# A gated cross-attention megakernel: the ternary layer written into the attention heads' plan, weights loaded first

## The chip, the cores and the metric

The kernel runs on one core of one Trainium2 chip, as one launch. The metric is the time of that launch on the device, in microseconds (us): 1436.66 us, the median of three runs (1432.61 to 1437.38). PE is TensorE, DVE is VectorE, ACT is ScalarE, POOL is GpSimd and SP is SyncE, whose queue issues most DMAs.

## What is computed

Two transformer-like layers on x of 16 tiles with 128 rows of 512 numbers, in float32. The change touches only the first layer, that is the first two lines of four:

```
x = x + tanh(g_xattn[0]) * heads(layernorm(x), ctx, mask)        # 16 heads of 32, 128 keys a tile
x = x + tanh(g_ffn[0])   * ternary(layernorm(x), weight, bias)   # one 512x512 layer
x = x + tanh(g_xattn[1]) * features(layernorm(x), ctx)           # sigmoid attention over features
x = x + tanh(g_ffn[1])   * experts(layernorm(x))                 # routing, 16 experts, shared expert

heads:   x = rmsnorm(h) * norm_w ; q = x wq', k = ctx wk', v = ctx wv'
         softmax(q k' / sqrt(32), masked) v ; then out wo' * sigmoid(x wg')
ternary: xn = x / rms(x); gamma = mean|weight| per output row
         w3 = clip(round(weight / (gamma + eps)), -1, 1)
         s  = max|xn| / 127 per row of x;  xq = clip(round(xn / (s + eps)), -127, 127)
         out = (xq w3') * gamma * s + bias
```

## The kernel before

The tensor x lies in SBUF as X, 16 tiles of 128x512. The stages run one after another, each as a block of the five engines' programs, and a block ends for all engines together.

**Start of the heads (lines 300 to 383, 449 to 470).** SP loads the five weights into two raw buffers in turn (qT and kT, not yet in use), so the third load waits until the first weight has been transposed; between them stand the loads of X (four of 1 MB), of two context tiles and of the masks. PE transposes each weight by 16 transposes into four PSUM banks (L351), ACT writes the high half of each quarter (L367) and DVE the low half (L211): a float32 number is used as a sum of two float32r halves, and `mm3` (lines 60 to 64) makes one product of three matmuls. After that a prologue does the first pair's transposes and the projections k and q.

**The heads' loop.** Tiles go in groups of four (GB = 4, NG = 4). One string, `plan` (lines 231 to 238), sets the order of a group, the same for all engines. A word is a step: `Sa`, `Sb` the scores of half a tile (four heads in each of two banks), `sm` the softmax of a quarter (DVE maximum L694, subtraction L699, ACT exponential L602, DVE row sums L707, one sum pass for two quarters), `pT` the transposes of the probabilities (PE L427, ACT L557), `pv` their product with v, `rc` and `bc` the reciprocals of the sums and their broadcast by PE, `on` and `oT` the normalised output and its halves, `v`, `g`, `oP`, `q`, `k` the projections, `xT`, `cT` the transposes of a tile of normalised x and of context (PE L427, ACT L555, DVE L627). PE writes transposes to two banks T in turn and projections to two banks M in turn; whoever is two steps later in the same bank waits until it has been read. Each engine executes in order. PE's program is written out for four groups (`for g in range(NG)`, L472); ACT, DVE, POOL and SP run a hardware loop of four turns (`Fori`), with register arithmetic ahead of each wait. As a loop's turn is the same for every g, the last turn also transposes and projects tiles of a next group, which wraps round to the first tiles and is never used.

**The ternary stage (`ternary_ffn`, lines 738 to 944).** A block of its own. DVE makes the means and scales of all 16 tiles (`row_scale`, lines 113 to 131, with two powers on POOL, L139 and L142), and the ternary weights (L809 to L822). Then it goes in pairs of tiles: normalise (L829), maximum (L832), three small steps (L836 to L838), round (L843), PE transposes (L917), ACT to bf16 (L893), PE four matmuls a tile (L941), DVE the product with the scales (L854), POOL two additions to X (L876 the bias, L881 the product), DVE the statistics for the next normalisation (L859).

Of the kernel before, what the change touches and what calls it, by code (L numbers as in the profile page):

```python
# [66 lines left out]
def program(nc, x, ctx_in, mask, g_x, g_f, norm_w, wq, wk, wv, wo, wg, fw, fb,  # L67
            gate_w, ebias, w1, w2, w3, sw1, sw2, sw3, out):
    with ExitStack() as top:
        def sb(name, shape, dt=F32):  # L70
# [74 lines left out]
def attention_heads(nc, c, x, g_x, g_f, fw, ctx_in, mask, norm_w, wq, wk, wv, wo, wg):  # L145

    X, identF = c["X"], c["identF"]
    with ExitStack() as st:
# [9 lines left out]
        W = [sb(f"W{n}", [P, 2, KC, D], F32R) for n in "qkvgo"]  # L158
        WQ, WK, WV, WG, WO = W
# [15 lines left out]
        rs = sb("rs", [P, D])  # L175
# [3 lines left out]
        upd = sb("upd", [P, 2, D])  # L179
        mask_u8 = sb("mask_u8", [NB, S], U8)  # L180
        mask_f = sb("mask_f", [NB, S])
        mask_all = sb("mask_all", [P, NB, S], U8)
        T, M, SC = bank("T", 2), bank("M", 2), bank("SC", 2)
        O, REC = bank("O", 1)[0], bank("REC", 1)[0]


        raw = [t_[:, :, :, :].rearrange("p a k t -> p (a k t)").rearrange("p (o k) -> p o k", o=KC) for t_ in (qT, kT)]
        names = [(WQ, wq, "norm"), (WK, wk, None), (WV, wv, None), (WG, wg, "norm"), (WO, wo, "gate")]

        def scale_of(how, kc):  # L190

            return nw[:, kc:kc + 1] if how == "norm" else hg[:, 0:1] if how == "gate" else 1.0
        w_in = [sem(f"w_in{i}") for i in range(2)]
        nw_in, mask_in, w_tr, w_hi, w_lo = sem("nw_in"), sem("mask_in"), sem("w_tr"), sem("w_hi"), sem("w_lo")
        powered, m_ready, m_tr, m_col, scales = sem("powered"), sem("m_ready"), sem("m_tr"), sem("m_col"), sem("scales")
        hg_ready, tg_ready, gates_bc = sem("hg_ready"), sem("tg_ready"), sem("gates_bc")
        x_in, g_in = [sem(f"x_in{q}") for q in range(NG)], sem("g_in")
        zeroed, consts, seen = sem("zeroed"), sem("consts"), sem("seen")

        def rows_stats(dve, q):  # L200
            dve.wait_ge(x_in[q], 16)
            for t in range(q * GB, (q + 1) * GB):
# [24 lines left out]
        plan = steps("Sa.0 xT.1.0 Sb.0 sm.0 sm.1 v.0 cT.1.0 xT.1.1 g.0 pT.0 cT.1.1 q.1.0 Sa.1 pT.1 Sb.1 sm.2 sm.3 "
# [7 lines left out]

        prologue = [(n, 2, i) for n, count in (("cT", GB // 2), ("k", KC), ("xT", GB // 2), ("q", KC)) for i in range(count)]  # L240

        T_KINDS, M_KINDS = ("xT", "cT", "pT"), ("q", "k", "v", "g", "oP")
        SPLIT, BY_ACT, BY_DVE = ("xT", "cT"), ("q", "k", "g"), ("v", "oP")

        def of(kinds, steps=None):
            return [s for s in (plan if steps is None else steps) if s[0] in kinds]

        def at(kinds, s):


            back = 0
            if s[0] in ("xT", "cT", "q", "k") and s[1] == 0:
                s, back = (s[0], 2, s[2]), 1
            elif s[0] in ("oP", "v", "g") and s[1] < 0:
                s, back = (s[0], s[1] + GB), 1
            elif s[0] == "pT" and s[1] < 0:
                s, back = (s[0], s[1] + NQ), 1
            some = of(kinds)
            return some.index(s) + 1 - back * len(some)

        def upto(kinds, sub, n):

            some = of(kinds)
            if n >= 0:
                return len([s for s in some[:n] if s[0] in sub])
            return len([s for s in some[:n] if s[0] in sub]) - len(of(sub))

        assert len(of(T_KINDS)) % 2 == 0 and len(of(M_KINDS)) % 2 == 0
        c_in = [sem(f"c_in{q}") for q in range(2)]
        mask_all_in = sem("mask_all_in")  # L270
        mrow_ready = Count(sem("mrow_ready"), GB, before=GB)
        x_norm = Count(sem("x_norm"), GB, before=2)
        t_fill = Count(sem("t_fill"), len(of(T_KINDS)), True, 4)
        t_hi = Count(sem("t_hi"), len(of(T_KINDS)), True, 4)
        t_lo = Count(sem("t_lo"), len(of(SPLIT)), True, 4)
        m_fill = Count(sem("m_fill"), len(of(M_KINDS)), True, 2 * KC)
        m_act = Count(sem("m_act"), len(of(BY_ACT)), True, 2 * KC)
        m_dve = Count(sem("m_dve"), len(of(BY_DVE)), True)
        s_fill = Count(sem("s_fill"), NQ)
        s_half = Count(sem("s_half"), NQ)  # L280
        s_out = Count(sem("s_out"), 3 * NQ, True)
        r_out = Count(sem("r_out"), GB, True)
        p_exp = Count(sem("p_exp"), NQ)
        pv = Count(sem("pv"), 3 * GB, True)
        o_norm = Count(sem("o_norm"), 2 * GB, True)
        o_hi = Count(sem("o_hi"), GB)
        o_lo = Count(sem("o_lo"), GB, True)
        added = Count(sem("added"), GB, True)
        HG = GB // 2
        GC = HG * S  # L290

# [4 lines left out]
        def tile_of(g, grp, j):  # L296

            return ((g + 1) * GB) % NB + j if grp == 2 else g * GB + grp * HG + j

        with nc.Block() as block:  # L300
            @block.sync
            def _(sp):
                sp.dma_start(gates[:, 0:2], g_x.rearrange("(a n) -> a n", a=1)).then_inc(g_in, 16)
                sp.dma_start(gates[:, 2:4], g_f.rearrange("(a n) -> a n", a=1)).then_inc(g_in, 16)
                with nc.allow_non_contiguous_dma(reason="512 scales once"):
                    sp.dma_start(nw[:, :], norm_w.rearrange("(k p) -> p k", p=P)).then_inc(nw_in, 16)
                for n, (_, w, _) in enumerate(names):
                    if n >= 2:
                        sp.wait_ge(w_tr, KC * (n - 1))
                    sp.dma_start(raw[n % 2][:, :, :], w.rearrange("(o p) k -> p o k", p=P)).then_inc(w_in[n % 2], 16)  # L310
# [1715 lines left out]
```

## Time and profile before

| what | us |
|---|---|
| median of three runs | 1436.66 |
| the profiled execution | 1438.92 |
| its span, first to last instruction | 1437.2 |
| start, to the first scores of the heads | 57.6 |
| heads' loop, four groups | 365.7 |
| from the heads' last matmul to the next stage's first transposes | 87.0 |
| all later stages | 926.9 |

In the first slice of 36 us the DMAs move 299 GB/s.

The page of the profile has a line for each engine's busy time in 40 equal slices of about 36 us: PE is at nine tenths or more in slices 3 to 11 and at four and five tenths in slices 13 and 14, where DVE is at nine. The mean granted clock of TensorE over the span is 0.94. Times in the rows are us from the span's start.

### The profile page before, as it was taken

Reading aid. Unit: us, or ns where it says so; the run is one execution under the profiler, and the core shown is the slowest. Engines: PE = TensorE matmul, PEld = TensorE weight load, DVE = VectorE, ACT = ScalarE, POOL = GpSimd, SP = SyncE. Lnnn points to the kernel's source line nnn. Section 1 sums busy time; section 2 is a strip of 40 time slices with the busy share of each in tenths; the row PEclk is TensorE's granted clock in tenths of the full one; section 3 lists DMA queues with packets and bytes.
Section 4 is the critical chain, followed back from the end, with each engine's and each line's share of the span. In section 5 each row is a group of like instructions: output and inputs, shape, how many; then the busy total and the mean of one; then the engine's idle time right before and its main releaser. Section 6 shows DMA issues by size and latency. Waiting matters only on the chain. (4 is left out here: it accounts for less than half of the span.)

```text
span 1437.2 us, 26164 instructions
## 1 busy us (share of the span) xinstructions
PE 1261.7 (88%) x7939; PEld 1058.4 (74%) x7944; DVE 761.4 (53%) x1393; ACT 521.0 (36%) x994; POOL 421.7 (29%) x487
## 2 busy tenths in 40 slices
PE   4899999999974579968997889679999989999992
PEld 3788888888863257745775677569999978998992
DVE  5555565565559979963666543334324543424340
ACT  3334333343322168843111112234334543434340
POOL 0100000000015665550003740124444434443442
PEclk8899999999997779979998999889999999999996
DMA  8000000000000011133000200356435665545456
GB/s 299 24 8 16 16 16 1 16 16 16 10 7 1 0 59 44 37 135 119 0 1 0 90 30 30 129 162 135 85 73 133 146 161 145 128 86 133 81 140 161
DMA packets 53297, 103.81 MB, mean 72 GB/s; under 512 B 4807, under 2 KB 20167, under 8 KB 53176
## 3 DMA queue, kind: packets, MB, share of 16 engines
q1 hardware_dynamic: 37608, 66.04, 14.0%
q0 software_dynamic: 15632, 36.97, 13.3%
q8 instruction: 40, 0.66, 0.2%
q14 instruction: 17, 0.14, 0.0%
HBM read 76.26 MB, written 30.93 MB: 75 GB/s over the span
## 5 line engine op out<-in xcount | busy, mean ns | idle before, releaser
L1876 PE MATMUL t_H<-m_W,t_xT 128*128 128x352 f32 x1632 | 285.7, 331 | 15.8 <-DVE m_W L1954 13.9
L1876 PEld LDWEIGHTS t_H<-m_W,t_xT 128*128 128x128 f32 x1632 | 267.2, 192 | 18.0 <-DVE m_W L1954 14.4
L1843 POOL DMA_INDIRECT acc_d<-t_ys,t_sid x68 | 109.4, 1609 | 281.7 <-ACT t_ys L1905 199.7
L408 POOL TENSOR_TENSOR X<-X,upd 128x512 f32 x16 | 20.5, 1281 | 352.1 <-DVE upd L685 352.1
L62 PE MATMUL t_Y<-m_W,t_hT 128*128 128x512 f32 (+1 forms) x207 | 88.5, 427 | 9.1 <-DVE t_hT L1999 6.1
L1921 ACT ACTIVATE t_sl<-t_H 128x352 f32<-128x352 f32 x68 | 31.5, 464 | 173.7 <-PE t_H L1876 173.7
L1975 DVE TENSOR_TENSOR t_h<-t_H,t_sl 128x352 f32<-128x352 f32 x68 | 35.6, 523 | 104.4 <-ACT t_sl L1921 98.6
L1997 DVE TENSOR_TENSOR t_hT<-t_TH,t_hT 128x256 fp32r<-128x256 f32 x68 | 28.8, 423 | 106.8 <-ACT t_hT L1942 105.7
L64 PE MATMUL t_Y<-m_W,t_hT 128*128 128x512 f32 (+1 forms) x207 | 82.8, 400 | 0.0
L63 PE MATMUL t_Y<-m_W,t_hT 128*128 128x512 f32 (+1 forms) x207 | 82.5, 398 | 0.0
L1905 ACT ACTIVATE t_ys<-t_Y,t_wcol 128x512 f32<-128x512 f32 x69 | 47.4, 686 | 95.7 <-PE t_Y L64 88.2
L1817 POOL DMA_INDIRECT t_xg<-rows_d,t_gid x72 | 71.2, 989 | 22.0 <-issue 21.8
L602 ACT ACTIVATE pr<-pr 128x512 f32<-128x512 f32 x64 | 40.4, 631 | 83.3 <-DVE pr L699 83.3
L694 DVE TENSOR_REDUCE mx<-SC 128x4 f32<-128x512 f32 x64 | 43.9, 686 | 46.8 <-PE SC L517 46.8
L1334 POOL TENSOR_SCALAR m_W<-m_W,bst 128x128 fp32r<-128x128 f32 x64 | 55.3, 883 | 27.9 <-PE eL L1398 27.8
L1729 DVE SCALAR_TENSOR_TENSOR X<-eY,tg,X 128x512 f32<-128x512 f32 x32 | 23.9, 751 | 63.3 <-PE eY L64 63.3
L557 ACT ACTIVATE pT<-T 128x512 f32<-128x512 f32 x64 | 38.1, 595 | 47.2 <-PE T L427 46.6
L1950 DVE TENSOR_TENSOR t_xT<-t_TX,t_xT 128x512 fp32r<-128x512 f32 x69 | 47.6, 690 | 12.0 <-issue 7.4
L62 PEld LDWEIGHTS t_Y<-m_W,t_hT 128*128 128x128 f32 (+1 forms) x207 | 39.5, 191 | 16.1 <-DVE m_W L1991 6.8
L699 DVE TENSOR_TENSOR pr<-SC,mx 128x512 f32<-128x512 f32 x64 | 44.3, 692 | 13.2 <-DVE mx L694 13.2
L1855 PE MATMUL t_TX<-identF,t_xg 128*128 128x128 f32 x276 | 42.3, 276 | 9.9 <-DMA t_xg<-rows_d,t_gid 9.6
L1453 ACT ACTIVATE ehT<-eh 128x512 fp32r<-128x512 f32 (+1 forms) x24 | 15.2, 632 | 97.6 <-DVE eh L1671 97.6
(379 smaller groups left out, 3263.0 us busy)
## 6 DMA issues: line engine op xcount, KB each, us to landing
m_r<-in_L_ffn_w_dram SPq DMA_DIRECT2D x26, 704.0 KB, 5.1
m_r<-in_L_ffn_w_dram SPq DMA_DIRECT2D x13, 512.0 KB, 6.9
aCX<-in_ctx_dram SPq DMA_DIRECT2D x20, 256.0 KB, 2.6
CT<-in_ctx_dram SPq DMA_DIRECT2D x9, 512.0 KB, 3.8
rows_d<-before_w SPq DMA_DIRECT2D x17, 256.0 KB, 2.0
X<-in_x_dram SPq DMA_DIRECT2D x4, 1024.0 KB, 11.8
acc_d<-X SPq DMA_DIRECT2D x4, 1024.0 KB, 4.2
m_r<-in_L_ffn_sw_dram SPq DMA_DIRECT2D x4, 704.0 KB, 5.5
```

The source lines that it names most:

```text
L62: pe.matmul(out, lhs(0), rhs(0), start=first, stop=False)
L63: pe.matmul(out, lhs(0), rhs(1), start=False, stop=False)
L64: return pe.matmul(out, lhs(1), rhs(0), start=False, stop=last)
L694: dve.tensor_reduce(mx[:, n % 2, :], sc, AX.X, ALU.max).then_inc(s_out.sem, 1)
L699: dve.tensor_tensor(pr[:, n % 2, :, :], sc, mx[:, n % 2, :].unsqueeze(2).to_broadcast([P, HQ, S]), ALU.subtract).then_inc(s_out.sem, 1)
L1334: i = pool.tensor_scalar(tab_a[t % SLOTS][:, k, :], iP.bitcast(F32), place_p[:, t, k:k + 1], None, ALU.is_equal)
L1817: pool.indirect_dma_start(out=xg[:, b, :], out_offset=None, in_=m["rows_d"][:, :], in_offset=bass.IndirectOffsetOnAxis(ap=gid[:, b:b + 1], ...
L1843: pool.indirect_dma_start(out=m["acc_d"][:, :], out_offset=bass.IndirectOffsetOnAxis(ap=sid[:, b:b + 1], axis=0), in_=ys[:, b, :], in_offs ...
L1855: x_ = pe.transpose(TX[:, k * P:(k + 1) * P], xg[:, b % UT, k * P:(k + 1) * P], identF[:, :])
L1876: x_ = pe.matmul(bk[b % 2][:, 0:I], xT[:, b % 2, jx, k, :], W13[:, jw, k, j, :], start=k == 0 and jx == jw, stop=k == KC - 1 and jx == 1)
L1905: act.activation(ys[:, (b - 1) % UT, :], Y[(b - 1) % 2][:, :], ACT.Copy, scale=wcol[:, (b - 1) % UT:(b - 1) % UT + 1]).then_inc(y_evac, 1)
L1950: dve.tensor_tensor(xT[:, b % 2, 1, :, :], TX[:, :].rearrange("p (k t) -> p k t", k=KC), xT[:, b % 2, 0, :, :].bitcast(F32), ALU.subtract) ...
```

## The change

`attention_heads` and `ternary_ffn` become one function and one block, `attention_heads_and_ternary`.

- Weights: the order is k, q, v, g, o. Each has a raw buffer of its own (tiles 4 to 15 of X for k, q and v; halves of qT, kT, pr and pT for g and o) and is loaded as four DMAs of 256 KB. No load of a weight waits for anything; X's tiles 4 to 15 are loaded when k, q and v have been transposed. The weights' transposes use the four banks SC, O, REC, and stand between the context's transposes and the k and q projections. The means and scales are made for tiles 0 to 3, 4 to 7 and 8 to 15; only the first is made ahead of the loop.
- The plan is written out for all 16 tiles on every engine, with constant waits. Steps for tiles beyond 15 are left out.
- The ternary layer's steps stand in the plan: `fq`, `ft`, `fg` (weights, in group 0), and for each tile `st` (statistics), `ra`, `rb`, `rd` (means and scales of a pair, with the two powers on POOL between), `u` (quantise), `uT` (transposes), `fm` (four matmuls, scaling, addition), `sf` (statistics). They share the banks T and M, one buffer u, one uT and one upd.
- The row sums are a DVE reduction in both kernels (L707 before, L762 after). One buffer for v and one for the output's reciprocals replace two.

```diff
-        with ExitStack() as both:
-            attention_heads(nc, parts, x, g_x, g_f, fw, ctx_in, mask, norm_w, wq, wk, wv, wo, wg)
-            ternary_ffn(nc, parts, fb)
+        attention_heads_and_ternary(nc, parts, x, g_x, g_f, fw, fb, ctx_in, mask, norm_w, wq, wk, wv, wo, wg)
...
+        start = ("W.k cT.0 cT.1 W.q sx.0 sx.1 sx.2 sx.3 xa.0 k.0.0 k.0.1 W.v xb.0 k.0.2 k.0.3 xd.0 nm.0 nm.1 W.g xT.0 xT.1 "
+                 "mk.0 mk.1 mk.2 mk.3 q.0.0 q.0.1 nm.2 nm.3 W.o q.0.2 q.0.3 ")
...
+            plan += steps(
+                f"Sa.0 xT.2 Sb.0 sm.0 sm.1 v.0 st.-2 st.-1 cT.2 ra.-1 xT.3 {d[0]} g.0 rb.-1 pT.0 cT.3 q.1.0 rd.-1 Sa.1 pT.1 Sb.1 "
+                f"sm.2 sm.3 mk.4 q.1.1 u.-2 {d[1]} pv.0 q.1.2 sf.-4 sf.-3 pT.2 uT.-2 u.-1 {d[2]} q.1.3 Sa.2 pT.3 rc.0 Sb.2 sm.4 sm.5 "
+                f"fm.-2 bc.0 pv.1 on.0 oT.0 k.1.0 uT.-1 {d[3]} k.1.1 pT.4 {d[4]} v.1 fm.-1 Sa.3 pT.5 Sb.3 sm.6 sm.7 mk.5 "
...
+                f"k.2.0 rb.0 pv.6 k.2.1 rd.0 u.0 pT.14 uT.0 u.1 g.3 pT.15 rc.3 oP.2 bc.3 pv.7 on.3 oT.3 fm.0 k.2.2 uT.1 k.2.3 fm.1 "
+                f"oP.3 ", g)
+        plan += steps("sf.-4 sf.-3 st.-2 st.-1 ra.-1 rb.-1 rd.-1 u.-2 uT.-2 u.-1 fm.-2 uT.-1 fm.-1 sf.-2 sf.-1", NG)
...
+                    elif kind in T_KINDS:
+                        tf = at(T_KINDS, s)
+                        wait(pe, t_hi, tf - 2)
+                        wait(pe, t_lo, up_to(T_KINDS, SPLIT, tf - 2))
...
+                        elif kind == "uT":
+                            pe.wait_ge(q_step, U_STEPS * (t + 1))
...
+                def quantise(t):
+                    wait(dve, t_fill, at(T_KINDS, ("uT", t - 1)))
+                    step(1, dve.tensor_scalar(u[:, :], X[:, t, :], c["mean"][:, t:t + 1], c["rstd"][:, t:t + 1],
+                                              ALU.subtract, ALU.mult))
+                    wait(dve, m_dve, at(BY_DVE, ("fm", t - 2)))
+                    step(2, dve.tensor_reduce(sc[:, k, 0:1], u[:, :], AX.X, ALU.max, apply_absolute_value=True))
+                    step(3, dve.tensor_scalar(sc[:, k, 1:2], sc[:, k, 0:1], 1.0 / 127.0, None, ALU.mult))
+                    step(4, dve.tensor_scalar(sc[:, k, 2:3], sc[:, k, 1:2], 1e-8, None, ALU.add))
+                    step(5, dve.reciprocal(sc[:, k, 3:4], sc[:, k, 2:3]))
+                    dve.tensor_scalar(u[:, :], u[:, :], sc[:, k, 3:4], ROUND, ALU.mult, ALU.add).then_inc(q_step, 1)
```

Numbers in the plan count within a group of four tiles; a negative one is a tile of the group before (`u.-2` in group 1 is tile 2). In `Sa`, `Sb` and `pv` they count half tiles, in `sm` and `pT` quarters.

The order on PE at the start, from the first transposes of a weight to the first projection. In the kernel before, all five weights come first (the last of them is shown), then the context:

```order
L351 MATMUL T<-identF,qT 128x128 x8
L351 MATMUL M<-identF,qT 128x128 x8
L355 MATMUL SC<-identF,mask_f 128x16
L415 UNCONDITIONAL_BRANCH
L427 MATMUL T<-identF,CT 128x128 x8
L62 MATMUL M<-cT,Wk 128x256
```

In the changed kernel two weights stand ahead of the first projection (k), and the other three between the projections:

```order
L451 MATMUL SC<-identF,fdg 128x16
L409 MATMUL SC<-identF,X 128x128 x8
L409 MATMUL O<-identF,X 128x128 x4
L409 MATMUL REC<-identF,X 128x128 x4
L423 MATMUL T<-identF,CT 128x128 x8
L409 MATMUL SC<-identF,X 128x128 x8
L409 MATMUL O<-identF,X 128x128 x4
L409 MATMUL REC<-identF,X 128x128 x4
L62 MATMUL M<-cT,Wk 128x256
```

The weights' transposes moved from one run ahead of everything to pieces, and three of the five moved behind the first projections.

The order on DVE at the end of a group, from the softmax of the last quarters (mx, pr, sums) to the heads' next update of X (upd). Before:

```order
L699 TENSOR_TENSOR pr<-SC,mx 128x512
L707 TENSOR_REDUCE sums<-pr 128x4 x2
L630 ISA
L630 TENSOR_SCALAR mrow<-mask_all 128x128
L55 REGISTER_ALU
L729 RECIPROCAL rec<-sums 128x16
L55 REGISTER_ALU x2
L685 SCALAR_TENSOR_TENSOR upd<-gs,M 128x512
```

In the changed kernel (tmp, rstd are the scales of a pair, fu the quantised tile, fsc its scale):

```order
L762 TENSOR_REDUCE sums<-pr 128x4 x2
L722 TENSOR_SCALAR mrow<-mask_g 128x128
L632 TENSOR_TENSOR tmp<-tmp 128x2
L633 TENSOR_TENSOR tmp<-tmp 128x2
L634 TENSOR_SCALAR tmp<-tmp 128x2
L640 TENSOR_TENSOR rstd<-tmp 128x2
L650 TENSOR_SCALAR fu<-X,mean,rstd 128x512
L653 TENSOR_REDUCE fsc<-fu 128x1
L654 TENSOR_SCALAR fsc<-fsc 128x1
L655 TENSOR_SCALAR fsc<-fsc 128x1
L656 RECIPROCAL fsc<-fsc 128x1
L657 TENSOR_SCALAR fu<-fu,fsc 128x512
```

Ten instructions of the ternary layer have come between the row sums and what followed them; the same six from L650 on come once more behind them, for the second tile of the pair.

The order on PE at the same place, from the k projection by the transposes of the probabilities (pr) to the gate's projection (Wg). Before:

```order
L62 MATMUL M<-cT,Wk 128x256
L63 MATMUL M<-cT,Wk 128x256
L64 MATMUL M<-cT,Wk 128x256
L427 MATMUL T<-identF,pr 128x128 x4
L62 MATMUL M<-Wg,xT 128x512
```

And in the changed kernel:

```order
L62 MATMUL M<-cT,Wk 128x256
L63 MATMUL M<-cT,Wk 128x256
L64 MATMUL M<-cT,Wk 128x256
L423 MATMUL T<-identF,pr 128x128 x4
L423 MATMUL T<-identF,fu 128x128 x4
L62 MATMUL M<-Wg,xT 128x512
```

Four transposes of the quantised tile fu have come ahead of the gate's projection; they wait for L657 of the rows above.

## Rows read from the trace of the kernel before

**Rows 1.** Windows by stage: us, busy by engine, PEclk, DMA share, GB/s.
```profile
57.60:423.30 365.70, 364.40 (x3328) 302.55 (x3328) 209.98 (x350) 141.56 (x272) 19.24 (x15) 1.00 0.04 13
423.30:510.30 87.00, 39.93 (x160) 21.94 (x163) 79.25 (x142) 13.65 (x24) 50.82 (x36) 0.72 0.02 6
```

**Rows 2.** Waits of PE in the heads' loop: total, times, longest.
```profile
PE T L427 <- issue: 1.2, 4, 0.3
```

**Rows 3.** Timeline of PE in the heads: start, us, instruction.
```profile
57.63 0.39 PE L507 MATMUL SC<-mrow,onesB 1*128 1x512 bf16 x2 [0.56 <-ACT qT L561]
...
158.72 0.63 PE L427 MATMUL T<-identF,CT 128*128 128x128 f32 x4
...
162.70 0.39 PE L62 MATMUL M<-xT,Wq 128*128 128x256 f32 x1
...
166.42 0.60 PE L427 MATMUL T<-identF,pr 128*128 128x128 f32 x4
...
222.80 0.39 PE L62 MATMUL M<-cT,Wk 128*128 128x256 f32 x1
...
226.53 0.60 PE L427 MATMUL T<-identF,pr 128*128 128x128 f32 x4
226.99 0.51 PE L62 MATMUL M<-Wg,xT 128*128 128x512 f32 x1
...
417.52 0.39 PE L62 MATMUL M<-cT,Wk 128*128 128x256 f32 x1
...
420.48 0.40 PE L62 MATMUL M<-Wo,oT 128*128 128x512 f32 x1
...
423.05 0.40 PE L64 MATMUL M<-Wo,oT 128*128 128x512 f32 x1
```

**Rows 4.** Timeline of DVE in the heads.
```profile
157.89 0.68 DVE L627 TENSOR_TENSOR xT<-T,xT 128x512 fp32r<-128x512 f32 x1
...
162.80 0.69 DVE L694 TENSOR_REDUCE mx<-SC 128x4 f32<-128x512 f32 x1 [2.09 <-PE SC L517]
...
165.81 1.47 DVE L707 TENSOR_REDUCE sums<-pr 128x4 f32<-128x512 f32 x2
...
225.91 1.47 DVE L707 TENSOR_REDUCE sums<-pr 128x4 f32<-128x512 f32 x2
```

**Rows 5.** Timeline of DVE in the ternary stage.
```profile
427.48 0.19 DVE L113 TENSOR_TENSOR mean<-bst 128x16 f32<-128x16 f32 x1 [0.90 <-PEq L300]
...
428.39 0.17 DVE L119 TENSOR_SCALAR tmp<-tmp 128x16 f32<-128x16 f32 x1
...
438.64 1.00 DVE L829 TENSOR_SCALAR fu<-X,mean,rstd 128x512 f32<-128x512 f32 x2
439.68 1.22 DVE L832 TENSOR_REDUCE fsc<-fu 128x2 f32<-128x1024 f32 x1
...
441.54 0.88 DVE L843 TENSOR_SCALAR fur<-fu,fsc 128x512 f32<-128x512 f32 x2
...
450.34 2.69 DVE L829 TENSOR_SCALAR fu<-X,mean,rstd 128x512 f32 x2
...
506.65 0.69 DVE L863 BATCH_NORM_STATS2 bst<-X 128x6 f32<-128x512 f32 x1 [0.35 <-POOL X L881]
```

**Rows 6.** Timeline of POOL: the power of 8 and of 16 tiles, one addition.
```profile
34.02 1.69 POOL L139 TENSOR_TENSOR tmp<-tmp,nhalf 128x8 f32<-128x8 f32 x1 [30.36 <-DVE tmp L119]
...
424.60 1.26 POOL L408 TENSOR_TENSOR X<-X,upd 128x512 f32 x1 [6.02 <-DVE upd L685]
428.64 2.91 POOL L139 TENSOR_TENSOR tmp<-tmp,nhalf 128x16 f32<-128x16 f32 x1 [2.79 <-DVE tmp L119]
```

**Rows 7.** Timeline of PE: two weights' transposes, and the ternary matmuls.
```profile
25.52 1.97 PE L351 MATMUL T<-identF,kT 128*128 128x128 f32 x8 [6.71 <-DMA kT<-in_L_xattn_wg_dram]
...
30.94 1.09 PE L351 MATMUL T<-identF,qT 128*128 128x128 f32 x8 [1.98 <-DMA qT<-in_L_xattn_wo_dram]
...
449.06 1.90 PE L941 MATMUL fM<-fwT,fuT 128*128 128x512 bf16 x8 [0.33 <-ACT fuT L893]
```

More of the change, by code:

```diff
@@ L261, in upto @@
[L261 to L272, printed above, removed]
@@ L282, in attention_heads @@
[L282 to L290, printed above, removed]
+                nums = [int(n) if n.lstrip("-").isdigit() else n for n in nums]
+                if kind in TILED:
+                    nums[0] += GB * g
+                    if not 0 <= nums[0] < NB:
+                        continue
+                elif kind in ("q", "k"):
+                    nums[0] += 2 * g
+                    if nums[0] >= NB // 2:
+                        continue
+                elif kind in ("Sa", "Sb", "pv"):
+                    nums[0] += 2 * GB * g
+                    if nums[0] >= NH2:
+                        continue
+                elif kind in ("sm", "pT"):
+                    nums[0] += NQ * g
+                    if nums[0] >= NU:
+                        continue
+                elif kind in ("ra", "rb", "rd"):
+                    nums[0] += 2 * g
+                    if not 0 <= nums[0] < NB // 2:
+                        continue
+                    nums[0] += FIRST
+                elif kind in ("xa", "xb", "xd"):
+                    kind = "r" + kind[1]
@@ new lines, in attention_heads_and_ternary @@
+        plan += steps("sf.-4 sf.-3 st.-2 st.-1 ra.-1 rb.-1 rd.-1 u.-2 uT.-2 u.-1 fm.-2 uT.-1 fm.-1 sf.-2 sf.-1", NG)
+        scaled = [slice(0, GB), slice(GB, 2 * GB), slice(2 * GB, NB)] + [slice(2 * p, 2 * p + 2) for p in range(NB // 2)]
+        SPLIT, T_KINDS = ("xT", "cT"), ("xT", "cT", "pT", "uT", "ft")
+        BY_ACT, BY_DVE = ("q", "k", "g", "fg"), ("v", "oP", "fm")
+        M_KINDS, X_UPD, STATS = BY_ACT + BY_DVE, ("oP", "fm"), ("sx", "st", "sf")
+        PV = ("pv", "bc")
+        order = {}
@@ new lines, in wait @@
+        def wait(eng, sem_, n):
+            if n > 0:
+                eng.wait_ge(sem_, n)
+        w_in = {n: sem(f"w_in_{n}") for n in ORDER}
+        g_in, nw_in, mask_in, mg_in, b_in, c_in, f_in = (sem(n) for n in (
+            "g_in", "nw_in", "mask_in", "mg_in", "b_in", "c_in", "f_in"))
+        x_in = [sem(f"x_in{q}") for q in range(NG)]
+        zeroed, consts, gates_bc, tg_ready, hg_ready, b_ready = (sem(n) for n in (
+            "zeroed", "consts", "gates_bc", "tg_ready", "hg_ready", "b_ready"))
@@ L292, in col_of, with ctx_after @@
+        o_norm, r_out, o_hi, o_lo = (sem(n) for n in ("o_norm", "r_out", "o_hi", "o_lo"))
+        added, biased, q_step, f_step = (sem(n) for n in ("added", "biased", "q_step", "f_step"))
+        U_STEPS, F_STEPS = 6, 8
+        RING = SC + [O, REC]
         def col_of(j, r):
             return (j // 2 * 2 + r % 2) * HQ + r // 2 * 2 + j % 2
[L296 to L298 removed]
+        def ctx_after(eng, s):
+            wait(eng, t_fill, at(T_KINDS, s))
@@ L337, in _, with weight @@
             @block.tensor
             def _(pe):
+                def weight(n):
+                    pe.wait_ge(w_in[n], 16 * KC)
+                    for kc in range(KC):
+                        f = KC * ORDER.index(n) + kc
+                        if f == 0:
+                            pe.wait_ge(tg_ready, 1)
+                        if f == 1:
+                            pe.wait_ge(m_col, 1)
+                        wait(pe, w_hi, f - len(RING) + 1)
+                        wait(pe, w_lo, f - len(RING) + 1)
+                        for oc in range(KC):
+                            i = pe.transpose(RING[f % len(RING)][:, oc * P:(oc + 1) * P], raw[n][oc][:, kc * P:(kc + 1) * P],
+                                             identF[:, :])
+                        i.then_inc(w_tr, 1)
@@ L401, in _ @@
-            @block.gpsimd
-            def _(pool):
-                added.grant(pool)
-                for half in range(2):
-                    row_power(pool, c, scales, powered, True, half)
-                def add(b):
-                    pool.tensor_tensor(X[:, g * GB + b, :], X[:, g * GB + b, :], upd[:, b % 2, :], ALU.add)\
-                        .then_inc(added.sem, 1)
-                with pool.Fori(0, NG) as g:
-                    for b in range(GB):
-                        m_dve.wait(pool, g, at(BY_DVE, ("oP", b)), c["passed_pool"])
-                        add(b)
```

1033 lines of the change are left out of this document (430 added, 603 removed), and 7 rows, old and new, of the table plan.

## The prediction, made before the changed kernel ran

> **What bounds the kernel now.** I read the windows by stage first, then PE's waits, then the timelines of PE, DVE and POOL at single places. In the heads' loop PE is busy 364.4 of 365.7 us and DVE 210.0 [rows 1]. The loop is at PE's rate: it waits for nothing but 1.2 us, 0.3 in each group [rows 2]. That 0.3 is before the first `pT` of a group, which needs a bank T that DVE reads only just before: here DVE has no slack at all. In the 87.0 us behind the heads DVE is busy 79.3 and PE 39.9, at a granted clock of 0.72 [rows 1]: that stretch is at DVE's rate. A stage at PE's rate with DVE half idle and a stage at DVE's rate are being laid over each other. PE's program was written out for four groups already, so writing out changes the registers and branches of DVE, ACT, POOL and SP, and PE gets no longer code.
>
> **The change part by part.** All is counted against the profiled execution, 1438.9 us (span 1437.2), which is 2.3 above the median of 1436.66.
>
> *Start.* The first scores are at 57.6 [rows 3]. PE stood waiting for loads there, 6.7 us for the gate's weight and 2.0 for the next [rows 7]. Now loads are queued without a wait, and the weights' transposes lie between projections. PE's work ahead of the first scores is 5 weights, 4 tiles' transposes and 8 projections. At the faster clock 8 transposes are 1.09 us [rows 7], a weight 2.2 and a tile about 0.5, and a q or k projection is 1.48 (two take 417.52 to 420.48 [rows 3]): 10.9 + 2 + 11.8 = 24.7 us. As the first matmul was at 7.7 and the mask is now waited for first, PE starts at about 8.5, so 33 is the earliest. In its order DVE has to make 20 quarter lows (0.7), 4 statistics (0.6), one set of scales (1.1 + two powers), 4 norms (0.5), 4 lows of tiles, and PE's q waits behind all of them; following this order through, I come to 42, with a few matmuls at the lower clock, where 8 transposes take 1.97 [rows 7]. Gain 15.6; bounds 0 (it stays at 57.6) and 24.
>
> *PE's added work in the heads.* A tile of the ternary layer is one set of transposes, 0.46 (226.53 to 226.99 [rows 3]), and four matmuls, 0.95 (8 in 1.90 [rows 7]): 1.4 us. Fourteen tiles go beside the heads, 19.6, and the ternary weights add about 1.4. Cost 21.0, all on the path, as PE has no idle time.
>
> *Dropped work.* The last group no longer transposes and projects for tiles that do not exist: 8 projections of 1.48 and 4 transposes of 0.45, 13.6 us. Gain 13.6, but see below.
>
> *Waits that PE gets for DVE.* First the lengths. Quantising a tile is 0.5 to normalise, 0.61 for the maximum, three small steps in about 0.6, 0.44 to round, and hops between: 2.3 us [rows 5]. The first part of a pair's scales is 1.1 (427.48 to 428.56 [rows 5]). A power is 1.69 for 8 columns and 2.91 for 16 [rows 6]; 2 columns are not shown, the line through the two gives 0.8 (bounds 0 and 1.69), to which I add 0.15 for the hops.
> (a) End of a group. DVE has finished the sums of the last quarters at 227.4 (225.91 + 1.47 [rows 4]). Behind these now stand the mask 0.1, `rb` 0.6, the second power 0.95, `rd` 0.2 and `u.0` 2.3, with the hop 231.7. PE comes to `uT.0` at 226.99 [rows 3] and waits 4.7 us. Behind it in PE's order is everything, the gate's projection first. Four times: 18.8.
> (b) `uT.-2`, groups 1 to 3. PE's scores end at 162.7 and it reaches this place after the transposes at 166.42, so at 166.9 [rows 3]. DVE finishes the sums at 167.3 [rows 4], then mask and `u.-2`: 169.7. Wait 2.8, three times: 8.5.
> (c) Start of groups 1 to 3. `xT.3` is read by DVE at 157.89 [rows 4] and PE needs its bank for `cT.3` at 158.72 [rows 3]. One more statistic (0.6) and `ra` (1.1) now stand ahead, so it ends at 160.3, not 158.6. Wait 1.7 with the hop, three times: 5.1.
> (d) `k.1.1` waits for the scaling of `fm.-2`, which stands behind two quarters' softmax on DVE: about 0.8, three times: 2.4.
> (e) Group 0 has instead the ternary weights (four times about 2.9 us on DVE) and 12 statistics. Most lie in DVE's idle time; where `fq.3`, four statistics and a scale come together (6.5 us) and ahead of `rc.0` it is late by 1 to 2 us: 3.5.
> (f) The last group. With the projections gone PE has less to do than DVE: followed through, half of the 13.6 is lost again, 7.0.
> Together 45.3 us. Bounds: 0, if DVE's steps fit in its 43% of idle time, and 70 if each is half as long again.
>
> *What remains behind the heads.* 87.0 us go from the last matmuls, at 423.3, to the next stage's first transposes; the last statistic ends at 507.3 (506.65 + 0.69 [rows 5]), so 84.0 to there and 3.0 more that stay. Now only the last pair is behind the heads: update 0.7, addition 1.3 [rows 6], statistic 0.7, `ra` 1.1, power, `rb`, power, `rd` 2.7, `u.14` and `u.15` 5.1, transposes and ACT 1.2, four matmuls 1.8 at the lower clock, update 0.8, addition 1.4, statistic 0.8, hops 0.7: 18.3. Gain 65.7. Row sums are on DVE in both kernels: 0. Fewer register instructions take up to 0.2 us from each maximum-to-subtraction step, which lies in the same DVE chains: counted 0, worth up to some 2 us a group.
>
> Sum: 1438.9 - 15.6 + 21.0 - 13.6 + 45.3 - 65.7 = 1410.3; against the median 1408.
>
> *A rule weighed.* Beside POOL's additions two normalisations take 2.69 us, alone 1.00 [rows 5], so 0.85 more each. The Trainium skill ("SBUF — State Buffer", SBUF: two separate sides) says that the port pair that VectorE and GpSimd share is an exclusive lock, held for a whole instruction; the row agrees. By that rule a `u` or `rd` that meets one of the 12 additions of a group waits for it; by the rows alone I took the undisturbed lengths. The additions follow `upd` and the first step of `u`, where DVE is mostly at maxima and at reads of PSUM; what it would cost if they met is the last rival.
>
> **The rivals.**
> 1. *DVE's work is hidden.* If PE waits for less than 15 us in all, the sum is 1408 - 45 = 1363 (with 15 us 1378). For it: DVE is idle 156 us in the loop [rows 1]. Against it: the places above are no shares but rows, and at (a) PE has only 4.2 us between the scores and `uT.0` where DVE has 8.7 us of work.
> 2. *The start gains nothing*, because every step of it waits for DVE's lows in order or for the X loads: 1408 + 15.6 = 1424. For it: 7 MB of weights, X and context must come in at the 299 GB/s of the page's first slice, which is 23 us, and DVE's chain is near the path. Against it: 8.7 us of PE's waits on loads are shown [rows 7] and go.
> 3. *The POOL additions hold VectorE where PE waits*; this one is slower. Before there were 4 additions in a group of the heads, now 12, of 1.28 us. If all hold DVE for their length on the path, 15.4 us a group, 61 in all: 1408 + 61 = 1469. It decides from 7 of 12 on (1408 + 36 = 1444). For it: the 2.69 us. Against it: 16 additions stand in the loop of before, and PE keeps its rate [rows 1, 2].
> 4. *The merge does not hide anything*, that is, PE waits for each ternary tile its whole DVE time: 14 tiles of 4.8 us (2.3 to quantise, 0.7 the update, 0.6 a statistic, 1.2 half a pair's scales) are 67 in place of 45: 1430, close to no change. Against it: DVE's idle time.
>
> **How the numbers follow.** My forecast (PE's waits between 15 and 60 us, the start gains 8 or more) has 0.58, its own range is 1380 to 1424. Rival 1 has 0.20, rival 2 0.11, rival 3 0.04, rival 4 0.04, the rest is for what I don't see. The range of 8 in 10 goes from 1370 to 1430: it takes in the upper part of rival 1, and rival 2 and leaves out rival 3. The runs before spread over 0.3%, and 0.3% is what can be told from no change, so 1432.3 and below is faster. Faster 0.91, same 0.04, slower 0.05.
>
> **What would show it.** The first scores at 42 us, the last matmuls of `Wo` near 460, the next stage's transposes at about 482. PE's waits in the heads: the longest on the quantised tile (fu), some 4.7 us at the group ends and 2.8 at `uT.-2`, then on DVE's reads of xT; DVE busy about 75 us in 100. I am wrong if PE's waits on fu are under 10 us in sum (rival 1), if the first scores are later than 50 (rival 2), or if the rounding or small steps of `u` or the norms are above 1 us beside POOL (rival 3). The stages behind should be unchanged within 2 us.

## The result and the profile after

The changed kernel takes 1420.5 us (median of four runs, 1417.49 to 1421.89), the kernel before 1437.02 (four runs). The ratio is 0.9878, with a 95% interval of 0.9859 to 0.9898: 1.2% or 17 us less. Forecast were 1408 and 29 us less, within 1370 to 1430. The profiled execution took 1417.49, the fastest of the four, with a span of 1415.8.

The windows by stage of the changed kernel: start, groups 0 to 3 (each to the transposes of its first quantised tile), the rest of the last group, the tail behind the heads, all later stages. Columns as in [rows 1].

```profile
0.00:40.50 40.50, 27.63 (x197) 26.71 (x199) 22.49 (x50) 18.44 (x35) 3.81 (x15) 0.96 0.79 276
40.50:132.90 92.40, 80.01 (x744) 66.62 (x745) 73.55 (x164) 35.67 (x70) 12.12 (x10) 1.00 0.08 22
132.90:240.20 107.30, 98.23 (x864) 79.87 (x865) 69.35 (x142) 38.21 (x72) 18.55 (x16) 0.98 0.04 12
240.20:348.60 108.40, 99.29 (x865) 80.79 (x865) 69.33 (x142) 38.21 (x72) 18.55 (x16) 0.97 0.04 11
348.60:451.70 103.10, 90.40 (x777) 71.14 (x777) 64.30 (x130) 34.14 (x62) 18.55 (x16) 0.93 0.01 1
451.70:468.30 16.60, 15.59 (x103) 11.80 (x104) 5.83 (x12) 3.40 (x6) 3.81 (x3) 0.82 0.01 1
468.30:492.30 24.00, 6.17 (x19) 2.33 (x18) 12.75 (x39) 1.19 (x2) 10.28 (x9) 0.56 0.08 22
492.30:1415.80 923.50, 826.64 (x4258) 706.17 (x4258) 441.40 (x828) 346.86 (x663) 343.38 (x420) 0.95 0.38 95
```

The start is 40.5 us in place of 57.6. The heads are 427.8 (40.5 to 468.3) in place of 365.7, at a mean clock below 1.00 from the second group on. What is left behind them is 24.0 in place of 87.0 [rows 1]. The later stages took 923.5 after 926.9, which no part of the change touches; it is as large as the scatter of the runs. These four differences are -17.1, +62.1, -63.0 and -3.4, together the span's -21.4. The second and third belong together: the heads and the ternary stage were 365.7 + 87.0 = 452.7 and are 427.8 + 24.0 = 451.8, so the merge in this order gave 0.9 us, and the start gave most of the gain.

PE's waits from 40.5 to 468.3 in the changed kernel, in total, times and longest, the longest totals only, answer to [rows 2], where there was 1.2 us:

```profile
PE T L423 <- DVE fu L657: 25.2, 7, 5.3
...
PE T L423 <- ACT pT L569: 4.5, 4, 1.6
...
PE REC L539 <- DVE rec L767: 3.7, 2, 2.0
```

The quantised tile (fu) is the first of them by far (an eighth wait for it, of 10.1 us, lies in the tail). PE's timeline at the places of term (a) in groups 0, 1 and 3 and of term (b) in groups 1 and 3, each with its wait in brackets, and matmuls behind two of them:

```profile
132.93 0.69 PE L423 MATMUL T<-identF,fu 128*128 128x128 f32 x4 [4.16 <-DVE fu L657]
...
172.83 0.63 PE L423 MATMUL T<-identF,fu 128*128 128x128 f32 x4 [2.51 <-DVE fu L657]
...
240.22 1.09 PE L423 MATMUL T<-identF,fu 128*128 128x128 f32 x4 [4.17 <-DVE fu L657]
240.97 0.78 PE L62 MATMUL M<-Wg,xT 128*128 128x512 f32 x1
241.54 0.63 PE L63 MATMUL M<-Wg,xT 128*128 128x512 f32 x1
241.97 0.63 PE L64 MATMUL M<-Wg,xT 128*128 128x512 f32 x1
...
388.29 0.63 PE L423 MATMUL T<-identF,fu 128*128 128x128 f32 x4 [2.38 <-DVE fu L657]
...
390.17 0.41 PE L62 MATMUL M<-xT,Wq 128*128 128x256 f32 x1
390.39 0.41 PE L63 MATMUL M<-xT,Wq 128*128 128x256 f32 x1
...
451.68 1.09 PE L423 MATMUL T<-identF,fu 128*128 128x128 f32 x4 [5.33 <-DVE fu L657]
```

The waits are 4.16 and 4.17 (5.33 in the last group) where 4.7 was forecast, and 2.51 and 2.38 where 2.8 was. What was not forecast stands behind the wait of 4.17: the matmuls of the gate's projection start 0.43 us after each other, where the output projection of the kernel before started them every 0.23 (420.48 to 423.05 in eleven steps [rows 3]). That is TensorE's lower clock, 1.2 in place of 2.4 GHz. The granted clock, in windows that begin with the end of each of the four waits at (a), is 0.50 to 0.64. The last line is a window behind the wait of 2.38, where the clock was low too:

```profile
132.90:137.00 4.10, 4.08 (x13) 3.34 (x14) 2.35 (x7) 0.60 (x1) 0.00 (x0) 0.58 0.00 0
240.20:244.00 3.80, 3.77 (x11) 3.22 (x12) 2.35 (x7) 0.60 (x1) 0.00 (x0) 0.50 0.00 0
348.60:353.00 4.40, 4.40 (x15) 3.71 (x16) 2.35 (x7) 0.60 (x1) 0.00 (x0) 0.64 0.00 0
451.70:458.00 6.30, 6.30 (x20) 5.05 (x21) 2.35 (x7) 0.73 (x2) 0.00 (x0) 0.53 0.02 4
390.00:396.00 6.00, 6.00 (x31) 3.87 (x30) 2.95 (x9) 0.98 (x2) 0.00 (x0) 0.50 0.01 3
```

### The profile page after: what moved, and what is told of

It is laid out like the page before. It is cut to its first block and busy times, and to the rows that moved or that the text cites. A ratio compares the mean times of both kernels' runs of the same rounds, so it can differ in the third digit from the quotient of the medians.

```text
span 1415.8 us, 25091 instructions
## 1 busy us (share of the span) xinstructions
PE 1244.0 (88%) x7821; PEld 1045.4 (74%) x7822; DVE 759.0 (54%) x1507; ACT 516.1 (36%) x982; POOL 429.0 (30%) x504
## 5 line engine op out<-in xcount | busy, mean ns | idle before, releaser
L1648 POOL DMA_INDIRECT t_xg<-rows_d,t_gid x72 | 71.5, 993 | 22.0 <-issue 21.4
L386 POOL TENSOR_TENSOR X<-X,upd 128x512 f32<-128x512 f32 x16 | 20.3, 1272 | 163.4 <-DVE upd L735 163.4
L373 POOL TENSOR_TENSOR tmp<-tmp,nhalf 128x2 f32<-128x2 f32 (+2 forms) x22 | 18.6, 846 | 150.1 <-DVE tmp L625 120.7
L1729 ACT ACTIVATE t_xT<-t_TX 128x512 fp32r<-128x512 f32 x69 | 41.3, 599 | 24.4 <-PE t_TX L1686 24.3
```

What stands on the lines that cost most here:

```text
L1648: pool.indirect_dma_start(out=xg[:, b, :], out_offset=None, in_=m["rows_d"][:, :], in_offset=bass.IndirectOffsetOnAxis(ap=gid[:, b:b + 1], ...
L1729: act.activation(xT[:, b % 2, 0, :, :], TX[:, :].rearrange("p (k t) -> p k t", k=KC), ACT.Copy).then_inc(tx_hi, 1)
```

## The experiments

Nine variants ran, one of them twice, and the changed kernel once more. Ratios are to the kernel before, timed in the same rounds; the three jobs gave it medians of 1436.5, 1436.88 and 1434.48 us. The changed kernel's 1420.5 is of another job than e1 to e4, so differences to it are given by the medians and, where they are not the same, by the ratios too. In the cuts of the plan, placeholders such as `{d[2]}` are left out, and `...` stands for unchanged words.

**The long wait taken away (e1).** Only two words of the plan move:

```diff
-    rd.0 u.0 pT.14 uT.0 u.1 g.3 pT.15 rc.3 oP.2 bc.3 pv.7
+    rd.0 u.0 pT.14 g.3 pT.15 rc.3 oP.2 uT.0 u.1 bc.3 pv.7
```

> The changed kernel, with the transposes of the first quantised tile of a group (uT.0) and the second quantisation (u.1) moved behind the output projection oP.2; nothing else. In the changed kernel PE waits there 4.16, 4.17, 4.16 and 5.33 us, and runs at half its rate for 3 to 6 us behind each wait. My theory (a wait of some 4 us costs its length and a stretch of slow clock): the four waits go, 17.8 us, with them about 8 us of slow clock, and about 2 come back as waits for the late oT.3: 24 us less than the changed kernel, ratio to before near 0.972. Rival one (the lateness of DVE only moves): the wait appears at the output projection oP.3 or the update behind it, less than 8 us are gained, ratio 0.983 or more. Rival two (the slow clock comes anyway): 16 us are gained and PE's clock is still about 0.97 in the heads, ratio 0.977.

1397.28 us, ratio 0.9743 (0.9713 to 0.9773), less than the changed kernel by 23 us in the medians and 19 by the ratios. The four waits are gone. Waits on fu are left at term (b), once 1.11 in the last group, and in the tail:

```profile
PE T L423 <- DVE fu L657: 17.7, 5, 9.1
PE M L62 <- issue: 6.9, 6, 1.9
```

The clock of the heads rose with it (0.99 from 40.5 to 449.0), though it was still low in three stretches of some 4 us, from 348.5, 376.0 and 444.0. Both rivals fall: the gain is the waits' 17.8 us and more. The second line shows what came back, 1.87 us in each of three groups, where k.2.3 needs the bank that DVE frees with the update of fm.0. That update is late in part because of POOL. In this order the rounding of u.1 falls beside an addition, and it takes 1.32 us where it took 0.49; DVE's row and POOL's at the end of group 1:

```profile
240.29 1.32 DVE L657 TENSOR_SCALAR fu<-fu,fsc 128x512 f32<-128x512 f32 x1
```

```profile
240.05 1.27 POOL L390 TENSOR_TENSOR X<-X,fbrow 128x512 f32<-128x512 f32 x1
```

That the excess over the waits is the clock is shown by the next kernel and not by this one.

**The wait kept, PE not idle in it (e2).**

```diff
                         elif kind == "uT":
+                            if t % GB == 0:
+                                for n_ in range(56 if t == NB - GB else 44):
+                                    pe.transpose(T[(tf - 1) % 2][:, n_ % KC * P:(n_ % KC + 1) * P], identF[:, :], identF[:, :])
                             pe.wait_ge(q_step, U_STEPS * (t + 1))
```

> The changed kernel, with 44 transposes of the identity (56 in the last group) issued by PE into the free bank while it waits for the first quantised tile of a group; their result is overwritten. The wait for DVE stays what it is, only PE is not idle in it. My theory (it is PE's idleness that costs the clock behind the wait): the gate's projection behind it runs at 0.23 us a matmul in place of 0.43, about 8 us less than the changed kernel, ratio to before near 0.982. Rival (the clock falls for another reason, or the extra work costs as much): no change within 2 us, ratio 0.988.

1411.12 us, ratio 0.9832 (0.9809 to 0.9855), less than the changed kernel by 9 us in the medians and 7 by the ratios, with 188 transposes added. PE's timeline at the end of the second group:

```profile
236.28 0.60 PE L423 MATMUL T<-identF,pr 128*128 128x128 f32 x4
236.71 4.97 PE L470 MATMUL T<-identF 128*128 128x128 f32 x44
241.51 0.60 PE L423 MATMUL T<-identF,fu 128*128 128x128 f32 x4
241.87 0.48 PE L62 MATMUL M<-Wg,xT 128*128 128x512 f32 x1
242.19 0.39 PE L63 MATMUL M<-Wg,xT 128*128 128x512 f32 x1
242.42 0.39 PE L64 MATMUL M<-Wg,xT 128*128 128x512 f32 x1
```

The transposes of fu still come 5.2 us behind those of pr (4.8 in the changed kernel), and the projection behind them runs at 0.23 us a matmul. So it is PE's idleness that costs the clock at these four places, and it costs 7 to 9 us over four waits that last 17.8 us together. My theory holds and the rival falls. The clock still fell behind the shorter waits that were left: in this execution it was low from 171.5 to 175.5, 281.0 to 291.5 and 390.0 to 394.0, behind the waits of 2.53, 2.51 and 2.39 at (b).

**Loads that wait again (e3).**

```diff
+                sp.wait_ge(w_tr, KC)
                 load_w("v")
                 load_masks(0)
+                sp.wait_ge(w_tr, 2 * KC)
                 load_w("g")
+                sp.wait_ge(w_tr, 3 * KC)
                 load_w("o")
```

> The changed kernel, but the loads of v, g and o wait until k, q and v have been transposed, as with two raw buffers; order, pieces and all else stay. My theory (part of the 17 us at the start is that loads no longer wait): PE waits on DMA again, about 8 us in all, and the first scores are at 46 to 50 in place of 40.5; ratio near 0.993. Rival (the gain is from laying projections between the weights alone): PE's waits fall into time that it waits for DVE's lows anyway, first scores within 2 us of 40.5, ratio 0.988.

1419.45 us, ratio 0.9869 (0.9851 to 0.9886): no change. The first scores are at 41.2, PE waits 0.7 us on a load. My theory falls and the rival holds: in this order, loading v, g and o only when k, q and v have been transposed is soon enough. "First and back to back" gives nothing here.

**The weights' transposes in one run (e5),** asked because e3 had left the start's 17 us without a cause:

```diff
-    W.k cT.0 cT.1 W.q sx.0 sx.1 sx.2 sx.3 xa.0 k.0.0 k.0.1 W.v xb.0 k.0.2 k.0.3 xd.0 nm.0 nm.1 W.g xT.0 xT.1
-    mk.0 mk.1 mk.2 mk.3 q.0.0 q.0.1 nm.2 nm.3 W.o q.0.2 q.0.3
+    W.k W.q W.v sx.0 sx.1 sx.2 sx.3 xa.0 W.g xb.0 W.o xd.0 cT.0 cT.1 nm.0 nm.1 k.0.0 k.0.1 k.0.2 k.0.3 xT.0 xT.1
+    mk.0 mk.1 mk.2 mk.3 q.0.0 q.0.1 nm.2 nm.3 q.0.2 q.0.3
```

> The changed kernel, but at the start the five weights' transposes stand in one run ahead of the context and the projections, in the order k q v g o; loads, buffers and pieces stay those of the change. Asks what gave the 17 us at the start, after loads that wait had cost nothing. Theory (it is the projections between the weights, which fill PE's waits for the weights' low halves): the first scores come at 46 to 52, 6 to 10 us later, ratio near 0.993. Rival (it is the four banks that belong to the weights alone, the loads in pieces and the shorter scales): the first scores stay within 2 us of 40.5, ratio 0.988.

1427.06 us, ratio 0.9929 (0.9911 to 0.9948), where the changed kernel on the same chip (after_again) had 1419.77 and 0.9882 (0.9861 to 0.9903). The first scores are at 50.8. PE's waits up to there:

```profile
PE SC L409 <- DMA X<-in_L_xattn_wv_dram: 3.6, 1, 3.6
PE SC L409 <- DVE Wg L691: 3.5, 1, 3.5
...
PE SC L409 <- DMA X<-in_L_xattn_wq_dram: 1.8, 1, 1.8
```

In one run PE waits for the loads even though they are queued back to back, and for DVE's lows. So the order, projections between the weights, gives 10 of the start's 17 us (7 of them in the total). The other 7, between this kernel's 50.8 and 57.6, were not taken apart: shorter scales, masks earlier, pieces of 256 KB, or banks of the weights' own.

> The changed kernel as it is, once more, on the chip of the next three: ratio 0.988, first scores at 40.5.

**The ternary tiles behind the heads (e4).** From the group's string u, uT, fm and sf are taken out, and behind the heads stands:

```diff
+        for t_ in range(NB + 2):
+            plan += [(k_, t_ - d_) for k_, d_ in (("u", 0), ("uT", 0), ("fm", 1), ("sf", 2)) if 0 <= t_ - d_ < NB]
```

> The changed kernel, but quantising, transposes, matmuls, update and last statistics (u, uT, fm, sf) of all 16 tiles stand behind the heads, in one pipelined run; the start, the pairs' scales and the ternary weights stay in the heads' plan. Tells what laying the ternary tiles beside the heads gives alone. My theory: the heads lose 19.6 us of PE's work and the waits on the quantised tiles with their slow clock (about 33), and take some 373 us in place of 428; behind them DVE needs about 4.5 us a tile, 72 in place of 24: some 7 us slower or faster than the changed kernel... as a number: the run behind is 76 us, so total 1417 + 52 - 55 = about 1415 to 1420, ratio 0.985 to 0.989. Rival (merging hides most of the ternary layer, and gives most of the gain): 20 us or more slower than the changed kernel, ratio over 1.0.

1466.94 us, ratio 1.0207 (1.0192 to 1.0221), 46 us slower than the changed kernel. The windows of the heads and of the run behind them:

```profile
40.20:417.00 376.80, 356.01 (x3240) 293.50 (x3240) 235.84 (x480) 141.68 (x268) 35.79 (x34) 0.99 0.04 12
417.00:541.00 124.00, 44.33 (x126) 20.68 (x128) 68.08 (x149) 9.55 (x16) 44.37 (x36) 0.54 0.01 4
```

The heads are 377 us, as expected (373): without the tiles they are 51 us shorter. The run behind is 124 in place of my 76, so the estimate of that half failed. With one buffer u, one uT and one upd, and the clock at 0.54, a tile is a chain of some 7 us, of which DVE works 4 (from one update to the next, 432.42 to 439.22, it waits 2.98 for the matmuls). The total that I expected, 1415 to 1420, failed, and the rival's number came; but its reason, that merging gives most of the gain, does not follow, since the run behind is slower than the stage that stood there before. Against this chain merging hides 46 us. Against the kernel before it is worth 0.9 us (452.7 and 451.8), and that includes the dropped work, 13.6 us as the prediction counted it. (377 + 87.0 = 464 would count the pairs' scales and the ternary weights twice, as both stretches make them.) So at this point of the study the merge had only moved the time from one place to the other, and moving steps in it (e1, e8) is what made it pay.

**The second kind of wait, first attempt (e6).** Besides the move of e1:

```diff
-    pT.2 uT.-2 u.-1 q.1.3 Sa.2 pT.3 rc.0 Sb.2 sm.4 sm.5 fm.-2 bc.0 pv.1 on.0 oT.0 k.1.0 uT.-1 k.1.1 pT.4 v.1 fm.-1 ... k.1.2
+    pT.2 q.1.3 Sa.2 pT.3 rc.0 Sb.2 uT.-2 sm.4 sm.5 u.-1 bc.0 pv.1 on.0 oT.0 k.1.0 k.1.1 fm.-2 pT.4 v.1 uT.-1 ... k.1.2 fm.-1
```

> uT.0 and u.1 behind oP.2 as in e1; and in groups 1 to 3 the transposes of the third quantised tile (uT.-2) behind the scores Sb.2, the fourth's quantisation (u.-1) behind the next two maxima, its transposes behind v.1, its matmuls behind k.1.2. Takes PE's other wait for a quantised tile away, 2.4 to 2.5 us three times (7.4). Theory (each such wait costs its length and little clock, as PE kept the fast clock behind these shorter ones): 6 to 8 us less than e1, about 1390, ratio 0.968 to 0.970. Rival (DVE is then late at another place, the scores or on.0): within 2 us of e1, ratio 0.974.

1403.66 us, ratio 0.9764 (0.974 to 0.9788): not faster than e1, its median 4 to 6 us higher. The waits of 2.5 are gone, and in each of groups 1 to 3 one of 3.2 to 3.3 us has come, PE waiting for ACT's copy of k (kT), with some 4 us of the lower clock behind it. PE's wait in group 1, then ACT's timeline, then DVE's:

```profile
177.41 1.25 PE L435 MATMUL M<-fwT,fuT 128*128 128x512 bf16 x3 [3.28 <-ACT kT L591]
```

```profile
172.51 0.58 ACT L600 ACTIVATE o<-REC 128x512 f32<-128x512 f32 x1
176.23 0.63 ACT L604 ACTIVATE oT<-o 128x512 fp32r<-128x512 f32 x1 [3.13 <-DVE o L771]
176.77 0.64 ACT L591 ACTIVATE kT<-M 128x256 f32<-128x256 f32 x2
```

```profile
173.24 0.54 DVE L650 TENSOR_SCALAR fu<-X,mean,rstd 128x512 f32<-128x512 f32 x1
...
175.11 0.49 DVE L657 TENSOR_SCALAR fu<-fu,fsc 128x512 f32<-128x512 f32 x1
175.51 0.68 DVE L771 TENSOR_TENSOR o<-O,o 128x512 f32<-128x512 f32 x1
```

The quantisation on DVE stands ahead of the normalised output (o), ACT waits 3.13 for that output, and behind it in ACT's order is the copy of k, without which PE gets no bank. The lateness had moved by way of a third engine, which in the heads of the changed kernel is busy 150 of 428 us.

**One word moved (e8), and more (e9).** e8 is e6 with `u.-1` behind `on.0 oT.0`:

```diff
-    sm.4 sm.5 u.-1 bc.0 pv.1 on.0 oT.0 k.1.0
+    sm.4 sm.5 bc.0 pv.1 on.0 oT.0 u.-1 k.1.0
```

> e6 with one word moved: the second quantisation (u.-1) stands behind on.0 and oT.0 on DVE, not ahead of them. In e6 PE waited 3.2 to 3.3 us in each of groups 1 to 3 for ACT's copy of k.1.0, which in ACT's order stands behind oT.0, which waits for DVE's on.0, behind u.-1. Theory (the lateness moved through ACT's order): those waits go, PE waits for no quantised tile inside the heads, and it is 6 to 8 us less than e1, 1390, ratio 0.968 to 0.970. Rival (each group is by now at DVE's own pace, wherever its steps stand): within 2 us of e1, ratio 0.974.

1391.2 us, ratio 0.9702 (0.9681 to 0.9724); e1 in the same job (e1_again) had 1399.86 and 0.9753 (0.9729 to 0.9777).

> e1 (uT.0 and u.1 behind oP.2) once more, on the chip of e8 and e9, so that they can be compared on one chip: ratio to before 0.974, 1397 us.

Nine us less than e1 (7 by the ratios), and PE's wait for kT at that place is 1.0 in place of 3.3, so the cause named for e6 holds, and the rival that a group is at DVE's pace falls. e9 moves three words more:

```diff
-    cT.2 ra.-1 xT.3 ... on.3 oT.3 fm.0 k.2.2 uT.1 k.2.3 fm.1 oP.3
+    cT.2 xT.3 ra.-1 ... on.3 oT.3 k.2.2 fm.0 k.2.3 uT.1 oP.3 fm.1
```

> e8, and the first part of a pair's scales (ra.-1) stands behind the transposes xT.3 rather than ahead, and at the end of a group fm.0 stands between k.2.2 and k.2.3 and fm.1 behind oP.3. Aims at the waits of 0.97 and 1.87 us a group that e1 still shows (cT.3's bank, and k.2.3's bank behind the update of fm.0). Theory: 2.5 us a group, 8 to 10 in all under e8, near 1382, ratio 0.963. Rival: they turn into waits elsewhere, within 2 us of e8.

1387.54 us, ratio 0.9682 (0.9662 to 0.9703), 4 us less than e8 in the median, with overlapping intervals: half of the 8 to 10 expected, and not clear of the noise. The wait of k.2.3 for its bank, in groups 0 and 1:

```profile
140.71 0.39 PE L62 MATMUL M<-cT,Wk 128*128 128x256 f32 x1 [1.05 <-ACT kT L591]
...
240.28 0.39 PE L62 MATMUL M<-cT,Wk 128*128 128x256 f32 x1 [1.04 <-ACT kT L591]
```

The 0.97 is gone, and 1.04 stands where 1.87 was. The wait in the tail grew from e8's 10.1 to 11.4, since fm.1 is now behind oP.3 there too: that took about 1 us back. It has the lowest median of this study, 3.2% under the kernel before and 2% under the changed one, the latter by the order of steps alone.

**The tail with PE busy (e7),** e6 with 96 transposes of the identity ahead of the wait for tile 14.

> e6, and behind the heads PE does 96 transposes of the identity (about 9 us) into the free bank while it waits for the quantised tile 14. Theory (idleness costs the clock in what follows): the tail's transposes and matmuls run at the fast clock, 2 to 3 us less than e6, and the next stage, which begins with a wait of 6 us for a load, gains nothing: ratio 0.002 below e6. Rival: the chain behind the heads is DVE's and POOL's, within 1 us of e6.

1402.97 us, ratio 0.9752 (0.9727 to 0.9777): within 1 us of e6, as the rival has it. The profile shows that the theory's mechanism was there all the same. The clock in the tail was 1.00 from 466.4 to 472.6, where e6 had 0.50 from 465.5 to 472.6. But the 96 transposes lasted 10.64 us, longer than the wait: from the last output projection on, the transposes of tile 14 came 1.2 us later than in e6 and the next stage's first transposes 0.5 us earlier, so the faster clock gave about 1.7 us and the overrun took most of it.

## Why the prediction was right where it was, and what it missed

The direction held, and three terms (the start, the waits, what is left behind the heads) held within 3 us. In the profiled executions, in us:

| term | forecast | measured |
|---|---|---|
| start | -15.6 | -17.1 |
| PE's added and dropped work | +7.4 | not apart |
| PE's waits in the heads | +45.3 | +43.1, sum of the 28 waits from 40.5 to 468.3 less the 1.8 that was there (1.2 and the first scores' 0.6) |
| slow clock behind the waits | none | +11.7: 8.6 behind the four at (a), 3.1 behind the 2.38 |
| rest of the heads | 0 | about 0, if the added and dropped work is as counted |
| behind the heads | -65.7 | -63.0 |
| later stages | 0 | -3.4 |
| sum | -28.6 | -21.4 |

**The start.** The number held, the reason only in part. I had named loads that no longer wait as what goes; e3 shows that they give nothing, and e5 that the order gives most. That the number came out near is in part luck.

**PE's waits for VectorE.** (a) was 4.2 for 4.7 in three groups: a power of two columns takes 0.70 us, not 0.8, and the maximum and the subtraction follow each other at 0.03 us, not 0.21, without the registers' arithmetic (rows 231.91 and 232.63 of the changed kernel's DVE below; the third row shows what DVE still waits for the power). (b) 2.5 for 2.8, (c) 0.64 and 0.97 for 1.7, (d) 0.44 for 0.8, in two groups. (e) was mis-sized: group 0 waits 8.3 us in six places, where I had 3.5. (f) 5.2 where I had 7.0 (0.81, 2.19 and 1.01, and the 1.17 by which the last (a) is above 4.16). So the sum of 45 was met by errors that nearly cancel. VectorE was busy 66 us in 100 in the heads (282.4 of 427.8), not 75.

```profile
231.91 0.69 DVE L751 TENSOR_REDUCE mx<-SC 128x4 f32<-128x512 f32 x1 [0.43 <-PE SC L517]
232.63 0.69 DVE L757 TENSOR_TENSOR pr<-SC,mx 128x512 f32<-128x512 f32 x1
...
237.52 0.16 DVE L640 TENSOR_TENSOR rstd<-tmp 128x2 f32<-128x2 f32 x1 [0.88 <-POOL tmp L373]
```

**The step that failed** is "Waits that PE gets for DVE": I took a wait to cost its length. Each wait of 4.16 us or more also cost 1.5 to 2.8 us of slow clock behind it (3 to 4 us of work at half rate behind the first and third, 6 behind the second and fourth), 8.6 in sum, against the 3.22 us from the transposes of fu to the next ones that e2 needs at the faster clock; e2 gave 7 to 9 back by keeping PE busy. The wait of 2.38 in group 3 cost 3.1 more: from it to the next transposes of fu 11.00 us pass, where group 1 needs 7.92. The rows that would have told me stand in the start of the kernel before: behind 6.7 us of waiting eight transposes took 1.97, behind 2.0 us 1.09 [rows 7], and the eight after those 1.77; I used them only as two speeds.

```profile
31.87 1.77 PE L351 MATMUL M<-identF,qT 128*128 128x128 f32 x8
```

The Trainium skill ("TensorE: Matmul & The Clock Gate", HAM oscillation) warns that idle gaps of PE make it start again at the lower clock each time. For the long waits the traces agree: in the four executions that have them (the changed kernel twice, e3 and e5), the clock was low behind all 16 waits of 4.14 us or more. For the short ones they agree only at times: of the 21 waits of 2.37 to 2.53 us at (b) in seven executions, 11 had a stretch of 4 to 11 us at the lower clock at them and 10 had none; the two executions of the changed kernel have one such stretch each, in group 3 and in group 2. What decides between the two is not shown here.

**Behind the heads.** Held within 3 us. The two tiles' matmuls and transposes ran at the lower clock, as counted.

**The rivals.** That DVE's work is hidden fell: 25.2 us of waits on fu in the heads, against the 10 named. So did the start that gains nothing. The POOL additions did not hold `u` in the changed kernel: the 16 normalisations took 0.532 to 0.548 us, the 16 roundings 0.485 to 0.489. That is in part luck of the order, since at the end of group 1 the addition ends at 239.60, just as the rounding begins (239.59). In e1, with `u.1` moved, it does hold VectorE (1.32 us, above), and in e4 the normalisation took 1.10 in the median and this rounding 1.29:

```profile
434.96 1.29 DVE L659 TENSOR_SCALAR fu<-fu,fsc 128x512 f32<-128x512 f32 x1
```

So the mechanism is real, and its weight was nothing in the changed kernel's order only.

**What stays open.** The part of the start between 50.8 and 57.6, what decides whether a wait of 2 to 2.5 us costs the clock, and the 5 us between the profiled executions' difference (21.4) and the medians' (17). The last places of the forecast came late too: the last matmuls of `Wo` end at 468, not near 460, and the next stage's transposes stand at 492, not 482.

## What to carry to other kernels

When a stage is laid into an order that already runs at one engine's rate, count no shares: go to each step that this engine now waits for, and sum what stands ahead of it on the other engines, from rows; that gave 45 us of waits where 43 came. Then add what an idle TensorE loses behind a wait, and look where a late step is queued on engines that have nothing to do with it, as ACT's copy of k in e6. Add up both sides of a merge: here 63.0 us went behind the heads and 62.1 came back in them. Once the waits are known, moving two words of the plan was worth more than the whole change had brought (19 to 23 us against 17).

## What the runs showed of the hardware

TensorE was at the lower clock behind waits of 4.16, 4.17, 4.16 and 5.33 us and stayed there for 3 to 6 us of full work; transposes of no use in such a wait (44 of them, 4.97 us, granted clock 1.00) kept it at the higher one, and the kernel became 7 to 9 us faster by doing more. Behind waits of 2.37 to 2.53 us it fell 11 times of 21, one execution of the same kernel differing from the next. A VectorE rounding of 128x512 took 0.49 us, and 1.32 when it met a GpSimd addition of 1.27. A GpSimd power of 2 columns took 0.70 us, of 8 columns 1.69 and of 16 columns 2.91 [rows 6].
